# Early loads for layer 1's routed experts, both DRAM sums begun at zero, and the residual added in the last stage

## The reference, cut to what matters

```
scores = sigmoid(x @ gate_w)                       # 64 experts
topk_ids = 6 best of (scores + bias) inside the 4 best of 8 groups
topk_w = 2.5 * scores[topk_ids] / sum(scores[topk_ids])
for each expert e, its first 96 tokens t:
    y[t] += topk_w * ((silu(x[t] @ w_gate[e]) * (x[t] @ w_up[e])) @ w_down[e])   # width 192
shared = (silu(x @ ws_gate) * (x @ ws_up)) @ ws_down
out = layernorm(x + y + shared)
```

## Time and profile before

| | us |
|---|---|
| median of 3 runs (1673.31 to 1678.6) | 1675.84 |
| the profiled execution | 1674.3 |
| its span, first to last instruction | 1672.6 |
| TensorE matmul busy | 1412.0 (84%) |
| DVE busy | 1059.7 (63%) |
| ACT busy | 699.6 (42%) |
| GpSimd busy | 619.9 (37%) |
| HBM traffic over the span | 142 GB/s |

### The profile page before, as it was taken

How to read it: one execution, slowest core, us unless ns; L and a number is a source line. 1 busy time by engine, 2 the same in 40 slices (tenths; PEclk the granted TensorE clock), 3 DMA queues, 4 the chain that set the end, 5 groups by cost and what they waited for, 6 DMA issues and landing times. The chain is left out here.

```text
span 1672.6 us, 23435 instructions
## 1 busy us (share of the span) xinstructions
PE 1412.0 (84%) x8185; PEld 1198.3 (72%) x8186; DVE 1059.7 (63%) x1837; ACT 699.6 (42%) x1123; POOL 619.9 (37%) x607
## 2 busy tenths in 40 slices
PE   5999869999699999944999789995888499999960
PEld 5787657776699999934899688884656377777750
DVE  4687646234476767636885556763582288888857
ACT  3221031000456565612554354440412188888850
POOL 1455500000322222132664333341064167878734
PEclk9999979999899999977999789996878599999995
DMA  4000040000788888833110100002411699999967
GB/s 158 1 1 26 26 129 0 1 1 0 247 278 285 272 282 280 264 134 90 51 51 1 32 1 1 26 26 73 139 38 51 230 339 337 346 345 343 349 166 301
DMA packets 112519, 239.25 MB, mean 143 GB/s; under 512 B 13481, under 2 KB 48297, under 8 KB 112443
## 3 DMA queue, kind: packets, MB, share of 16 engines
q1 hardware_dynamic: 84699, 169.55, 29.4%
q0 software_dynamic: 18784, 51.39, 11.2%
q10 hardware_dynamic: 8960, 17.30, 2.7%
HBM read 187.49 MB, written 50.72 MB: 142 GB/s over the span
## 5 line engine op out<-in xcount | busy, mean ns | idle before, releaser
L1049 POOL COPY e_index<-r_token_of 128x2 int32 (+1 forms) x31 | 8.1, 261 | 369.2 <-POOLq L602 203.6
L66 PE MATMUL bank<-e_xt_hi,e_w_hi 128*128 128x256 f32 x496 | 142.6, 287 | 0.0
L68 PE MATMUL bank<-e_xt_hi,e_w_lo 128*128 128x256 f32 x496 | 139.9, 282 | 0.0
L67 PE MATMUL bank<-e_xt_lo,e_w_hi 128*128 128x256 f32 x496 | 139.8, 282 | 0.0
L2389 POOL DMA_INDIRECT e_xg<-rows,r_token_of x64 | 116.5, 1820 | 31.2 <-issue 19.2
L1150 DVE TENSOR_TENSOR e_w_lo<-e_raw,e_w_hi 128x2048 fp32r<-128x2048 f32 x31 | 71.0, 2292 | 85.3 <-ACT e_w_hi L1107 85.3
L2397 POOL DMA_INDIRECT sums<-e_y,r_target_of x64 | 94.8, 1481 | 70.4 <-ACT e_y L2496 29.4
L2506 DVE TENSOR_TENSOR e_w_lo<-e_w_raw,e_w_hi 128x1536 fp32r<-128x1536 f32 x56 | 98.5, 1758 | 30.2 <-issue 15.2
L67 PEld LDWEIGHTS bank<-e_xt_lo,e_w_hi 128*128 128x128 f32 x496 | 93.9, 189 | 0.0
L66 PEld LDWEIGHTS bank<-e_xt_hi,e_w_hi 128*128 128x128 f32 x496 | 93.9, 189 | 0.0
L68 PEld LDWEIGHTS bank<-e_xt_hi,e_w_lo 128*128 128x128 f32 x496 | 93.7, 189 | 0.0
(11 more groups left out here) (455 smaller groups left out, 4651.6 us busy)
## 6 DMA issues: line engine op xcount, KB each, us to landing
e_w_raw<-in_w_gate_up SPq DMA_DIRECT2D x56, 768.0 KB
e_raw<-in_rw SPq DMA_DIRECT2D x62, 512.0 KB
e_w_raw<-in_w_down SPq DMA_DIRECT2D x32, 768.0 KB
e_raw<-in_rg SPq DMA_DIRECT2D x31, 512.0 KB
results<-e_y ACTq DMA_DIRECT2D x31, 512.0 KB, 5.1
rows<-resid SPq DMA_DIRECT2D x8, 1024.0 KB, 4.3
r_w_first<-in_w_gate_up SPq DMA_DIRECT2D x8, 768.0 KB
resid<-in_x SPq DMA_DIRECT2D x4, 1024.0 KB, 13.5
```

The lines of the kernel that those rows point to most:

```text
L66: pe.matmul(out, a_hi, b_hi, start=start, stop=False)
L67: pe.matmul(out, a_hi, b_lo, start=False, stop=False)
L68: return pe.matmul(out, a_lo, b_hi, start=False, stop=stop)
```

## The change

The weights of experts 0 to 5 (gate-up) and of their three pairs (down) get buffers that are placed over the transposed tokens `xt_hi` and `xt_lo`. SP loads them in the shared block as soon as the last gate-up step is done; expert 0's gate-up weights are loaded where they were. GpSimd gathers the rows of experts 0 to 3 there too, once the table stands, and the gathers of experts 4 to 7 begin the routed block. Both DRAM sums begin at zero, so that no residual is written, and GpSimd's wait for them moves ahead of its first scatter. In the last block GpSimd adds the first sum to the residual (`add_first`), one step ahead of DVE, which then adds the second. `ys` has two tiles, the down tiles alternate between banks 6 and 7, while `at_row` has three buffers instead of four. TensorE's table, which also uses bank 7, waits until all of `ys` has been copied.

```diff
@@ experts1_shared @@
+    with ExitStack() as before:
+        xt_hi, xt_lo = (k.sb("s1_xt_" + n, [P, KD, T], F32R, before) for n in ("hi", "lo"))
+    k.w1_early = [k.w1_first] + [rt(f"w1_early{p}", [P, KD, 2 * F1]) for p in range(1, 7)]
+    k.w2_early = [rt(f"w2_early{q}", [P, 3, D]) for q in range(3)]
+    k.xg_early = [rt(f"xg_early{p}", [CAP, D + E1]) for p in range(4)]
...
-        NR = 4
+        NR = 3
...
-        last_bank = [bank[6], bank[0], bank[1], bank[2]]
+        down_bank = lambda i: bank[6 + i % 2] if i < NT - TC else (bank[6], bank[0], bank[1], bank[2])[i - NT + TC]
@@ experts1_shared, SP @@
-                for c in range(NC):
-                    sp.dma_start(k.sums[1][0:T, :].rearrange("(c j p) d -> c p j d", p=P, j=TC)[c],
-                                 zeros.unsqueeze(1).to_broadcast([P, TC, D])).then_inc(k.s_sums1, 16)
...
+                for sums in k.sums:
+                    for c in range(NC):
+                        sp.dma_start(sums[0:T, :].rearrange("(c j p) d -> c p j d", p=P, j=TC)[c],
+                                     zeros.unsqueeze(1).to_broadcast([P, TC, D])).then_inc(k.s_sums, 16)
+                    sp.dma_start(sums[T:T + CAP, :], zeros[0:CAP]).then_inc(k.s_sums, 16)
...
-                sp.wait_ge(k.s_rows, 2 * 16 * NC)
-                for c in range(NC - 1):
-                    sp.wait_ge(s_res, TC * (c + 1))
-                    sp.dma_start(k.sums[0][0:T, :].rearrange("(c j p) d -> c p j d", p=P, j=TC)[c],
-                                 k.x[:, c * TC:(c + 1) * TC, :]).then_inc(k.s_sums0, 16)
+                sp.wait_ge(s_gu, NU)
+                for e in range(6):
+                    if e:
+                        sp.dma_start(k.w1_early[e][:, :, :].rearrange("p b n -> p (b n)"), io["w_gate_up"][e]).then_inc(k.s_w1_early[e], 16)
+                    if e % 2 == 0:
+                        sp.dma_start(k.w2_early[e // 2][:, :, :].rearrange("p f n -> p (f n)"), io["w_down"][e // 2]).then_inc(k.s_w2_early[e // 2], 16)
@@ experts1_shared, GpSimd @@
-                        pool.tensor_tensor(k.x[:, i, :], ys[:, :], k.x[:, i, :], ALU.add).then_inc(s_res, 1)
+                        pool.tensor_tensor(k.x[:, i, :], ys[:, i % 2, :], k.x[:, i, :], ALU.add).then_inc(s_res, 1)
...
+                pool.wait_ge(s_gu, NU)
+                pool.wait_ge(s_shared, 16)
+                pool.wait_ge(s_tab, 1)
+                for e in range(4):
+                    pool.indirect_dma_start(k.xg_early[e][:, :], None, k.rows1, bass.IndirectOffsetOnAxis(k.token_of[:, e:e + 1], 0)
+                                            ).then_inc(k.s_xg_early[e], 16)
@@ experts1_shared, TensorE @@
                     if c == NC - 1:
+                        pe.wait_ge(s_ys, NT - TC)
                         table()
...
-                        if i and i <= NT - TC:
-                            pe.wait_ge(s_ys, i)
+                        if 2 <= i < NT - TC:
+                            pe.wait_ge(s_ys, i - 1)
@@ experts1_shared, ScalarE @@
-                        if i:
-                            act.wait_ge(s_res, i)
-                        act.activation(ys[:, :], bank[6][:, :], ACT.Copy).then_inc(s_ys, 1)
+                        if i >= 2:
+                            act.wait_ge(s_res, i - 1)
+                        act.activation(ys[:, i % 2, :], down_bank(i)[:, :], ACT.Copy).then_inc(s_ys, 1)
@@ experts1_shared, DVE @@
-                    vec.wait_ge(k.s_sums1, 16 * (NC + 2))
@@ experts1_routed @@
-                pool.wait_ge(k.s_sums0, 16 * NC)
-                pool.wait_ge(k.s_sums1, 16 * (NC + 2))
-                for g in range(-6, E1 + 1):
+                for g in range(-2, E1 + 1):
                     if g + 6 < E1:
                         gather((g + 6) // U, (g + 6) % U)
+                    if g == 1:
+                        pool.wait_ge(k.s_sums, 2 * 16 * (NC + 1))
...
-                act.dma_start(k.sums[0][T - CH:T, :].rearrange("(j p) d -> p j d", p=P), k.x[:, NT - TC:NT, :]).then_inc(k.s_sums0, 16)
@@ combine1 @@
-                    sp.dma_start(k.x[:, c * NL:(c + 1) * NL, :], tiles(k.sums[0][0:T, :])[c]).then_inc(s_a[c], 16)
-                    sp.dma_start(other[:, c * NL:(c + 1) * NL, :], tiles(k.sums[1][0:T, :])[c]).then_inc(s_b[c], 16)
+                    sp.dma_start(first[:, c * NL:(c + 1) * NL, :], tiles(k.sums[0][0:T, :])[c]).then_inc(s_a[c], 16)
+                    sp.dma_start(second[:, c * NL:(c + 1) * NL, :], tiles(k.sums[1][0:T, :])[c]).then_inc(s_b[c], 16)
@@ combine1, GpSimd @@
+                def add_first(c):
+                    t = slice(c * NL, (c + 1) * NL)
+                    pool.wait_ge(s_a[c], 16)
+                    pool.tensor_tensor(k.x[:, t, :], k.x[:, t, :], first[:, t, :], ALU.add).then_inc(s_one, 1)
+
+                add_first(0)
                 for c in range(NG):
+                    if c + 1 < NG:
+                        add_first(c + 1)
@@ combine1, DVE @@
-                    vec.wait_ge(s_a[c], 16)
                     vec.wait_ge(s_b[c], 16)
-                    vec.tensor_tensor(k.x[:, t, :], k.x[:, t, :], other[:, t, :], ALU.add).then_inc(s_sum, 1)
+                    vec.wait_ge(s_one, c + 1)
+                    vec.tensor_tensor(k.x[:, t, :], k.x[:, t, :], second[:, t, :], ALU.add).then_inc(s_sum, 1)
```

More of the change, by code:

```diff
@@ L1899, in experts1_shared @@
     k.target_of = rt("target_of", [CAP, E1], I32)
-    k.s_sums0, k.s_sums1 = k.sem("e1_first_sums_begun"), k.sem("e1_second_sums_begun")
+    k.s_sums = k.sem("e1_sums_zeroed")
     k.w1_first = rt("w1_first", [P, KD, 2 * F1])
-    k.s_w1_first = k.sem("e1_gate_up_loaded0")
+    with ExitStack() as before:
[3 more added lines that the diff above has]
+    k.xg_early = [rt(f"xg_early{p}", [CAP, D + E1]) for p in range(4)]
+    rt("early_rest", [P, 2 * KD * T - 9 * KD * 2 * F1 - 4 * (D + E1)])
+    k.s_w1_early = [k.sem(f"e1_gate_up_loaded{p}") for p in range(7)]
+    k.s_w2_early = [k.sem(f"e1_down_loaded{q}") for q in range(3)]
+    k.s_xg_early = [k.sem(f"e1_rows_gathered{p}") for p in range(4)]
     with ExitStack() as ctx:
@@ L1909, in experts1_shared @@
         bias = sb("bias", [P, E1])
-        xt_hi, xt_lo = sb("xt_hi", [P, KD, T], F32R), sb("xt_lo", [P, KD, T], F32R)
         si, up = sb("si", [HF1, CH]), sb("up", [HF1, CH])
@@ L1913, in experts1_shared @@
         h_hi, h_lo = sb("h_hi", [HF1, 2, CH], F32R), sb("h_lo", [HF1, 2, CH], F32R)
-        ys = sb("ys", [P, D])
+        ys = sb("ys", [P, 2, D])
         scores = sb("scores", [P, NT, E1])
@@ L2089, in down @@
                     for i in range(4 * c, 4 * c + 4):
-                        if i and i <= NT - TC:
-                            pe.wait_ge(s_ys, i)
-                        out = last_bank[i - NT + TC] if c == NC - 1 else bank[6]
+                        if 2 <= i < NT - TC:
+                            pe.wait_ge(s_ys, i - 1)
+                        out = down_bank(i)
                         t = slice(i % 4 * P, (i % 4 + 1) * P)
@@ L2319, in _ @@
                     vec.wait_ge(s_dn, i + 1)
-                    vec.tensor_tensor(k.x[:, i, :], last_bank[j][:, :], k.x[:, i, :], ALU.add).then_inc(s_last, 1)
+                    vec.tensor_tensor(k.x[:, i, :], down_bank(i)[:, :], k.x[:, i, :], ALU.add).then_inc(s_last, 1)
                 vec.wait_ge(s_last, TC)
@@ L2345, in experts1_routed @@
         sem = lambda n: k.sem("e1_" + n)
-        s_w = [k.s_w1_first] + [sem(f"gate_up_loaded{p}") for p in range(1, U)]
-        s_v = [a for a in [k.sem(f"e1_down_loaded{q}") for q in range(U // 2)] for _ in range(2)]
-        s_g = [k.sem(f"e1_rows_gathered{p}") for p in range(U)]
+        s_w = k.s_w1_early + [sem(f"gate_up_loaded{p}") for p in range(7, U)]
+        s_v = [a for a in k.s_w2_early + [sem("down_loaded3")] for _ in range(2)]
+        s_g = k.s_xg_early + [sem(f"rows_gathered{p}") for p in range(4, U)]
         s_zero, s_wt = sem("hidden_zeroed"), sem("weights_kept")
@@ L2364, in load @@
                 def load(h, p):
+                    if not past(h, p, 6):
+                        return
                     e = U * h + p
@@ L2537, in combine1 @@
     with ExitStack() as ctx:
-        other = k.sb("c1_other", [P, NT, D], F32, ctx)
+        first, second = (k.sb("c1_" + n, [P, NT, D], F32, ctx) for n in ("first", "second"))
         s_a, s_b = ([k.sem(f"c1_{n}_loaded{c}") for c in range(NG)] for n in ("first", "second"))
-        s_sum = k.sem("c1_summed")
+        s_one, s_sum = k.sem("c1_first_added"), k.sem("c1_second_added")
         s_stat, s_var, s_rstd, s_ln, s_st = (k.sem("c1_" + n) for n in ("stats", "var", "rstd", "normed", "stored"))
```

16 lines of the change are left out of this document (7 added, 9 removed).

## The result

The changed kernel takes 1648.67 us, median of 4 runs (1647.79 to 1650.95), against 1675.14 for the kernel before (4 runs): ratio 0.9833 [0.9817, 0.9848]. The profiled spans are 1646.8 and 1672.6 us.

What follows compares the result with a forecast made beforehand. Bounds: the matmul engine in the routed stage, DVE in the last, with a 23.9 us hole and shared-stage waits ahead. Hole -19.2, shared stage -9, last stage +15 sum to -13.2 us, giving 1662.6 us; range 1650 to 1673.

Steps and rivals of the forecast that it cites:

- part 3: Last stage: GpSimd's additions and rstd and DVE's totals and applies exclude each other, 5.5 us per pair; 15 us later.
- GpSimd does add 0 and add 1 back to back ... +4.4: Last stage's start: DVE's first total waits for two GpSimd additions, beginning 4.8 instead of 0.4 us after the landing.
- the four terms: Shared stage: residual add 1.5, lost waits and restarts 5, clock 3.5, table -0.9; 9 us earlier.
- the table's -0.9: Shared stage: one at_row buffer fewer puts one more DVE product on the table's path, costing 0.9 us.
- one residual add slip ahead: Shared stage, before down-projection 1: one GpSimd residual add gets in front of DVE's table products, gaining 1.5 us.
- Part 1: Hole before the routed stage: early weights, early gathers and zero-begun sums bring the first transpose 19.2 us earlier.
- some 15 us of slack: Routed stage's end: weight loads run about 15 us ahead of need, so starting TensorE earlier costs nil.
- A: Last stage: exclusion costs little as additions slip beside statistics; stage +3, total -25, 1650.6 us; 20%.
- C: Last stage: DVE and GpSimd wait each other out, period 7.9 us, stage +33, total +5, 1681 us; 8%.
- B: Shared stage: ends where it did, since DVE's table work and GpSimd set it; total -4.2, 1671.6 us; 13%.
- D: Routed stage: becomes DMA-bound with TensorE starting earlier, 10 us of gain come back; total -3, 1672.6 us; 6%.

Runs made afterwards that it cites:

- half_add: The changed kernel with GpSimd's last-stage addition done for only one tile of each pair (128x512, output incomplete); 1642.63 us.
- no_rstd: The changed kernel without GpSimd's reciprocal deviation (var and power) and its wait for the statistics in the last stage; 1654.62 us.
- after_again: The changed kernel itself, unaltered, measured again beside a version with the old residual path and last stage, on the same chip; 1650.66 us.
- one_ys: The changed kernel with one ys tile and bank 6 alone again for the down tiles of chunks 0 to 2; 1662.58 us.
- before_wait_moved: The kernel before, with GpSimd's wait for both sums moved to its first scatter and DVE's wait for the zeros removed; 1673.61 us.
- late_loads: The changed kernel with the eight early weight loads issued only at the routed block's start, early gathers kept; 1659.53 us.
- late_gathers: The changed kernel with the early gathers moved to the routed block's start, early weight loads kept; 1655.42 us.
- rstd_first: The changed kernel with GpSimd's reciprocal deviation of each pair placed ahead of its addition for the next pair; 1666.44 us.

## Why the prediction was wrong

**The step that failed** is in part 3: "Per pair the additions, applies and `rstd` then exclude each other: 2.36 + 1.22 + 0.97 + 0.23 + 0.72 = 5.5 us". It measured 4.07. The 1.43 us between them: `rstd`'s two instructions run beside applies and total without lengthening the period (0.95); the addition's ends overlap the total by 0.17 more than a strict sum allows, the applies by 0.23 and the next total by 0.08 (from one total's end, the addition ends 2.19 later, the applies 0.74, the next total 1.14: 4.07). The 0.08 are DVE's own: in the kernel before, the total also begins 0.08 ahead of the applies' end (1663.93 against 1663.04 + 0.97). half_add shows the sum false by itself, 3.76 against 4.41. The Trainium skill, page "SBUF — State Buffer", section "SBUF: two separate sides", has the lock held for a whole instruction. The trace agrees where operations meet (3.31 for 0.97 in no_rstd) but not to the end: even without `rstd` the three would need 4.55, 4.47 with DVE's own overlap, and 4.07 is measured, so the measurement decides. The same row that I read, 1.98 us for the power beside a total, comes out as 0.85 in the kernel after in nearly the same place (0.22 us ahead of a total), and as 1.98 in half_add (0.20 ahead). What decides between them was not found.

**The start of that stage** was the second mis-sized term: "GpSimd does add 0 and add 1 back to back ... +4.4". DMA had not yet delivered tile pair 1: GpSimd waited 2.04 us for it (1610.53), so DVE's first total got in between, and began 6.17 us after the first load instead of 5.02, +1.15. The third total was at +3.5 (forecast 6.3) and the five periods after it cost 5 x 0.31 = 1.6 (forecast 8.7). The +3.5 holds some variation: the third total came 11.8 us after the first load in before, 12.9 and 13.3 in the two other executions of the old stage, 15.3 in after and 14.7 in after_again. Together +5.1 instead of +15: 9.9 of the 14.9 us by which the segments from the shared stage on fell below the sum.

**The shared stage** made 4.2 more, 13.2 instead of 9. Of the four terms, the table's -0.9 held (from its first matmul to the last down-projection 14.95 us instead of 13.98). Down-projection 1 began 3.65 us earlier in its stage, not 1.5. I had let one residual add slip ahead. Now all four are ahead: GpSimd's last one ends at 1226.47, before the first product at 1228.71, where before two of them took 7.11 and 6.81 us beside the products, and both hidden products came after. After the second product's end 1.17 us pass instead of 8.17; the products' end comes 3.35 us later in its stage. From there to the table it is 10.2 us shorter (40.25 to 30.03) against 8.5 forecast. As forecast, down-projection 1 begins at the low clock level: TensorE's matmuls start 0.43 us apart up to 1249.96 and 0.23 apart from 1250.27 on, and the 13.4 us around down-projection 1 have a clock of 0.81 and no idle time, against 0.50. I did not split this between waits and clock; one_ys shows that both hang on the second `ys`: there, too, the clock around down-projection 1 is 0.51.

**Part 1 was right**, 19.5 against 19.2, and so was the claim that the routed stage pays nothing for it: it kept its 287.9 us. But one reason under it was wrong and one was left open. I called the DMA side "some 15 us of slack" in the kernel before. Its windows show DMA full till late in the stage (347 GB/s in 1559 to 1590), and before_wait_moved, which starts TensorE 10.5 us earlier, paid 5.8 us at once; an estimate from these two is 5 us of slack. The rival "routed stage becomes DMA-bound" was therefore a real danger, and the 6.3 MB moved ahead of the stage kept it off (late_loads: +9.05). And I didn't divide the gain among the edits. Moving the wait took 10.5 us off the hole (before_wait_moved, 13.34 left); the early gathers are the other 9.1 (late_gathers, 13.39 left); the early weights are none of the hole (late_loads, 4.30) and pay in the routed stage alone.

**The rivals.** A, at 20%, has the outcome: exclusion costs little in the last stage (+5 where it said +3), and its reason, that additions slip beside statistics, is the mechanism shown. Its number, 1650.6, was near also by luck: the larger shared gain made up for the 2 us. My argument against it, "2.36 is longer than that", compared an addition with the statistics as a whole, when only the excess, 2.34 - 1.7 = 0.6 us, can cost. C (hand to hand, 7.9) is what rstd_first comes close to (6.82), and B and D did not occur. With A at 20% at the very edge of the range (1650), the range was too narrow on that side.

## What to carry to other kernels

When two engines share a resource for some of their operations, don't add up the excluded operations: lay both queues side by side on a time axis and count only the part of each operation that finds no unlocked stretch of the other engine to lie beside; the order within a queue decides that (4.07, 6.82 and 8.25 us per period from the same additions). When a hole in front of a bandwidth-full stage is closed, the bytes have to move with it: moving the wait alone took 10.5 us off the hole and 0.24% off the kernel; with the gathers and weights moved too, the hole lost 19.5 us and the routed stage kept its length. And when only one part of a scheme pays, try it without the other: the old residual path behind the new wait was 5.4 us better still.

## What the runs showed of the hardware

A GpSimd addition of 128x1024 float32 takes 2.34 us alone (rstd_first), where the straight line gave 2.36; six back to back beside DVE took 16.47 (no_rstd), and two DVE applies beside them 3.31 instead of 0.97, one whole addition more. DVE's statistics beside the same additions kept their length (0.69 and 0.66). Taking GpSimd's small `rstd` work out made a stage 5.3 us slower. The core's DMA moved 344 to 349 GB/s of weight loads, gathers and scatters together in every long window in which it was full. And one that stays open: the same 128x2 power took 0.85 (after) or 1.98 us (before, half_add) beside a total that began 0.20 to 0.22 us after it.
